# Sage layer behind the second layer's sums, and gathers issued half a round ahead of the maxima

## What is computed

```python
h = jnp.maximum(_layernorm(x), 0.0);  x = x + _L0_gnn_ref(h, adj, ...)   # GAT: 8 heads, then one output head
h = jnp.maximum(_layernorm(x), 0.0);  x = x + _L1_gnn_ref(h, adj, ...)   # GraphSAGE with the maximum over neighbours
h = jnp.maximum(_layernorm(x), 0.0);  x = x + _L2_gnn_ref(h, adj, ...)   # GAT, 4 heads
h = jnp.maximum(_layernorm(x), 0.0);  x = x + _L3_gnn_ref(h, adj, ...)   # mean over neighbours

# _L1_gnn_ref, the layer that the change is about
adj_ns = adj * (1.0 - eye)                       # no self loops
mx = where(adj_ns > 0, h[:, None], -1e30).max(axis=2)
neigh_agg = where(has_neigh, mx, h)              # a node without neighbours takes its own row
out = h @ W_self + b_self + neigh_agg @ W_neigh + b_neigh
out = relu(layernorm(out) * gamma + beta)
```

## Time and profile before

| | before |
|---|---|
| median of 3 runs | 9122.6 us (9110.27 to 9135.99) |
| the profiled execution, its own time | 9111.52 us |
| its span | 9109.8 us |
| busy PE, DVE, ACT, POOL | 5148.5, 5894.4, 4402.1, 5128.1 us |
| waits of PE's sage transposes for the maxima | 1096.9 us in 6 |
| POOL: gathers into G, into best | 1416 x 1061 ns, 1024 x 1068 ns |
| POOL: fetches of indices | 433 x 599 ns |

### The profile page before, as it was taken

The page is one execution under the profiler, slowest core; times in us unless marked ns, Lnnn a source line. Parts: engine busy times, 40 slices in busy tenths (PEclk is TensorE's granted clock), DMA queues, the critical chain, the costliest instruction groups (busy, mean ns, idle before and its releaser), DMA issues.

```text
span 9109.8 us, 178961 instructions
## 1 busy us (share of the span) xinstructions
PE 5148.5 (57%) x60584; PEld 4779.8 (52%) x60584; DVE 5894.4 (65%) x7002; ACT 4402.1 (48%) x3608; POOL 5128.1 (56%) x5234
## 2 busy tenths in 40 slices
PE   3673750365765668365865667556845667362026
PEld 3672750364755557363865567555745567361025
DVE  5874860386867788486867687687847688581024
ACT  5644730165635566165735566356715566160034
POOL 0004777377764677377764677276764677377630
PEclk9885875687877878687987888788877888686568
DMA  2114332234332533135322433234322433132210
GB/s 99 43 34 124 66 66 25 46 69 113 61 63 65 122 65 80 19 76 133 67 62 66 119 66 83 58 75 101 69 48 66 120 65 80 54 55 58 23 26 29
DMA packets 307180, 629.05 MB, mean 69 GB/s; under 512 B 113553, under 2 KB 165906, under 8 KB 270610
## 3 DMA queue, kind: packets, MB, share of 16 engines
q0 software_dynamic: 91936, 161.87, 16.9%
q1 hardware_dynamic: 212354, 456.38, 14.2%
q10 hardware_dynamic: 2160, 0.06, 0.0%
HBM read 506.89 MB, written 111.15 MB: 68 GB/s over the span
## 4 chain that ended last, share of the span: by engine, by line
POOL 20%; issue 16%; DVE 14%; PE 13%; DMA 8%; ACT 4%; POOLq 2%; DVEq 2%; ACTq 1%; SPq 0%
DMA G<-table,idx 6%; POOL G L552 6%; POOL best L552 5%; PE ps L1413 4%; POOL best L538 4%; PE ps L1386 3%; PE ps L1415 2%; POOL best L535 2%; DVE keys L1077 2%; POOL G L535 2%; ACT Pbuf L689 1%; PE ps L1438 1%; DVE key L1067 1%; POOL best L537 1%; ACT Hn L689 1%
## 5 line engine op out<-in xcount | busy, mean ns | idle before, releaser
L552 POOL DMA_INDIRECT G<-table,idx x1416 | 1502.7, 1061 | 508.5 <-issue 452.7
L1415 PE MATMUL ps<-Hn,AT 128*128 128x99 bf16 x12288 | 1774.5, 216 | 0.0
L1415 PE MATMUL ps<-X,AT 128*128 128x99 bf16 x12288 | 1735.0, 214 | 52.6 <-issue 52.6
L544 POOL DMA_DIRECT2D idx<-lists x433 | 259.3, 599 | 2445.9 <-issue 1964.9
L689 ACT ACTIVATE Hn<-Rb,q 128x2048 int8<-128x2048 f32 x768 | 1485.4, 1988 | 86.6 <-PE ps L1415 82.1
L689 ACT ACTIVATE Pbuf<-Rb,q 128x2048 int8<-128x2048 f32 x768 | 1487.8, 1987 | 18.2 <-PE ps L1415 15.6
L552 POOL DMA_INDIRECT best<-table,idx x1024 | 1093.7, 1068 | 319.4 <-issue 309.3
L1415 PEld LDWEIGHTS ps<-X,AT 128*128 128x128 fp8e4 x12288 | 1243.2, 101 | 57.6 <-issue 57.6
L1415 PEld LDWEIGHTS ps<-Hn,AT 128*128 128x128 fp8e4 x12288 | 1256.5, 102 | 0.0
L1413 PE MATMUL ps<-X,Hn 128*128 128x198 bf16 x6144 | 933.6, 268 | 567.6 <-DVE Hn L937 358.6
L1413 PE MATMUL ps<-Hn 128*128 128x198 bf16 x6144 | 960.3, 272 | 433.0 <-DVE Zs L957 236.0
(11 more groups left out here) (186 smaller groups left out, 11171.7 us busy)
## 6 DMA issues: line engine op xcount, KB each, us to landing
Rb<-in_adj SPq DMA_DIRECT2D x128, 1024.0 KB, 6.3
Rb<-rrows SPq DMA_DIRECT2D x104, 1024.0 KB, 6.3
bytes_A<-A SPq DMA_DIRECT2D x128, 256.0 KB
bytes_AT<-AT SPq DMA_DIRECT2D x128, 256.0 KB
AT<-bytes_AT SPq DMA_DIRECT2D x128, 256.0 KB, 3.6
AT<-bytes_A SPq DMA_DIRECT2D x128, 256.0 KB, 4.6
G<-table,idx POOLq DMA_INDIRECT x1416
h<-Hn SPq DMA_DIRECT2D x16, 1024.0 KB, 4.1
```

The source lines that it names most:

```text
L544: pool.dma_start(idx[:, slot, :], lists[bass.ds(r, 1)].rearrange("o p k -> (o p) k")).then_inc(idx_in[slot], 16)
L552: pool.indirect_dma_start(out=dst[:, k, :], out_offset=None, in_=table, in_offset=bass.IndirectOffsetOnAxis(ap=idx[:, slot, k:k + 1], axis ...
L1415: ins = pe.matmul(both[:, 0, 0:G], A8[:, jb, at], v[:, 0:G], start=False, stop=jb == T - 1, skip_group_check=True)
```

## The change

Two things change together.

In GpSimd's program `best` now takes the rows of every round, and `G`, half as wide, holds the maxima. Indices of a list are fetched in two transfers of four columns. A tile's rounds run by halves: wait for a half's four gathers (`landed`), fetch the same half's indices of the next list, take the half's maximum into `G` (the first half of a tile is a copy), then wait for those indices and issue the half's next four gathers (`ask`). The next list may be the next tile's first. The last tile of a graph runs its further rounds without this lead. The tree has two steps (2 and 1).

In `beside` the sage pairs come behind all 16 steps of the second layer's sums on PE (`sage`). On DVE the pairs' sums are handed to `finish`, which does one behind each of its operations from the third on; `statistics(1)` comes next, then the sage statistics as a loop, then `joined`. On ACT the exponential of `finish` stands behind the fourth of the eight sage copies, and `norm(1)` ahead of the sage norms. The three parts of the list stand behind steps 1, 2 and 3. The diff, cut to its core; the removed lines of `tile` are those printed above.

```diff
-        G = sb("G", [P, KEYS, F])
-        idx = sb("idx", [P, 2, KEYS], U32)
+        G = sb("G", [P, KEYS // 2, F])
+        idx = sb("idx", [P, KEYS], U32)
...
-            def fetch(r, slot):
+            def half(part):
+                return slice(part * (KEYS // 2), (part + 1) * (KEYS // 2))
+            def fetch(r, part):
                 plain(pool)
                 pool.wait_ge(list_in, r * 16 + 32)
-                pool.dma_start(idx[:, slot, :], lists[bass.ds(r, 1)].rearrange("o p k -> (o p) k")).then_inc(idx_in[slot], 16)
-            def rows_of(fetched, slot, dst):
+                pool.dma_start(idx[:, half(part)], lists[bass.ds(r, 1), :, half(part)].rearrange("o p k -> (o p) k")).then_inc(idx_in[part], 16)
+            def ask(r, part):
                 plain(pool)
-                pool.wait_ge(idx_in[slot], fetched * 16)
+                pool.wait_ge(idx_in[part], r * 16 + 16)
                 settle(pool)
-                for k in range(KEYS):
+                for k in range(part * (KEYS // 2), (part + 1) * (KEYS // 2)):
                     pool.indirect_dma_start(
-                        out=dst[:, k, :], out_offset=None, in_=table,
-                        in_offset=bass.IndirectOffsetOnAxis(ap=idx[:, slot, k:k + 1], axis=0)).then_inc(got[k], 16)
+                        out=best[:, k, :], out_offset=None, in_=table,
+                        in_offset=bass.IndirectOffsetOnAxis(ap=idx[:, k:k + 1], axis=0)).then_inc(got[part], 16)
+            def landed(r, part):
+                plain(pool)
+                pool.wait_ge(got[part], r * 64 + 64)
...
             def tile(b, t, last):
                 lo, hi = number(b, t), number(b, t + 1)
+                v = Chain(pool, merged, lo * MERGE, MERGE)
+                for part in range(2):
+                    landed(lo, part)
+                    if not last:
+                        settle(pool)
+                        fetch(lo + 1, part)
+                        plain(pool)
+                    if part == 0:
+                        settle(pool)
+                        v(pool.tensor_copy(G[:, :, :], best[:, half(0), :]))
+                    else:
+                        greater(v, G[:, :, :], best[:, half(1), :])
+                    if not last:
+                        ask(lo + 1, part)
+                settle(pool)
+                pool.sem_inc(merged, MERGE - v.n)
                 with pool.Fori(lo + 1, hi) as r:
+                    w = Chain(pool, merged, r * MERGE, MERGE)
                     if last:
+                        for part in range(2):
+                            fetch(r, part)
+                        for part in range(2):
+                            ask(r, part)
+                    for part in range(2):
+                        landed(r, part)
+                        if not last:
+                            settle(pool)
+                            fetch(r + 1, part)
+                            plain(pool)
+                        greater(w, G[:, :, :], best[:, half(part), :])
+                        if not last:
+                            ask(r + 1, part)
+                    w.end()
                     settle(pool)
                 v = Chain(pool, tree, (b * T + t) * TREE, TREE)
+                for width in (2, 1):
+                    greater(v, G[:, 0:width, :], G[:, width:2 * width, :])
                 settle(pool)
+                v(pool.tensor_copy(Agg[:, bass.ds(t, 1), :].rearrange("p o f -> p (o f)"), G[:, 0, :]))
                 v.end()
                 settle(pool)
...
-                fetch(number(b, 0), 0)
+                first = number(b, 0)
+                for part in range(2):
+                    fetch(first, part)
+                for part in range(2):
+                    ask(first, part)
                 with pool.Fori(0, T - 1) as t:
                     tile(b, t, False)
...
                 if b is not None:
                     prepare(LB, b)
                 if other is not None:
-                    sage_operands(other)
+                    sage_operands(other, range(T // 4))
+                if b is not None:
+                    elu_exp(LB, b, 0)
+                if other is not None:
+                    sage_operands(other, range(T // 4, T // 2))
+                if b is not None:
+                    norm(1, b, X, Hn, ACT.Relu)
+                if other is not None:
                     norm(4, other, Y, Y, ACT.Identity)
                     norm(2, other, X2, Hn2, ACT.Relu)
-                if b is not None:
-                    elu_exp(LB, b, 0)
-                    norm(1, b, X, Hn, ACT.Relu)
...
-            def finish(L, hn, lone):
+            def finish(L, hn, lone, between):
                 s, C = S[L], L.C
+                waiting = list(between)
+                def beside_it():
+                    if waiting:
+                        waiting.pop(0)()
...
                 v(dve.tensor_tensor(Z[:, full * w:], Z[:, full * w:], ps[:, full, 0:T * C - full * w], ALU.add))
+                beside_it()
                 v(dve.reciprocal(rden[:, :], zt[:, :, L.D]))
+                beside_it()
                 v(dve.tensor_tensor(o, o, rden[:, :].rearrange("p (t o) -> p t o", o=1).broadcast_to([P, T, L.D]), ALU.mult))
...
                 v(dve.tensor_tensor(X[:, :, :], X[:, :, :], Hn[:, :, :], ALU.add))
+                beside_it()
                 v.end()
+                while waiting:
+                    beside_it()
...
             def beside(b, other):
-                rest_of = []
-                between = [] if other is None or b is None else list(zip((0, 1, 2), list_tile(b, LIST_LB)))
-                if other is not None:
-                    for p in range(T // 2):
-                        between.append((p + 4, lambda p=p: sage_sums(other, p)))
-                        between.append((p + 5, lambda p=p: sage_statistics(other, p)))
-                    between.append((T // 2 + 4, lambda: rest_of.append(deviations(4, other))))
-                    between.append((T // 2 + 5, lambda: rest_of[0]()))
+                products = [] if other is None else [lambda p=p: sage_sums(other, p) for p in range(T // 2)]
                 if b is None:
-                    for at, work in sorted(between, key=lambda part: part[0]):
+                    for work in products:
                         work()
                 else:
                     prepare(LB, b)
-                    weigh(LB, 0, (b + 1) * 16, slice(0, 1), b, between)
+                    weigh(LB, 0, (b + 1) * 16, slice(0, 1), b,
+                          () if other is None else list(zip((1, 2, 3), list_tile(b, LIST_LB))))
+                    finish(LB, b, lone, products)
+                    statistics(1, b, X)
                 if other is not None:
+                    plain(dve)
+                    dve.wait_ge(M["sage"]["ev"], other * T + (T + 2))
+                    statistics(4, other, Y)
                     joined(other)
-                if b is not None:
-                    finish(LB, b, lone)
-                    statistics(1, b, X)
...
-            def sage_step(b, jb):
-                if jb == 1:
-                    sage_arrived(b)
-                if 2 <= jb < T // 2 + 2:
-                    sage_product(b, jb - 2)
-                if 1 <= jb < T // 2 + 1:
-                    sage_turned(b, jb - 1)
-            def sums(L, hn, other):
+            def sage(b):
+                sage_arrived(b)
+                for p in range(T // 2):
+                    sage_turned(b, p)
+                    sage_product(b, p)
+            def sums(L, hn):
...
                 if b is None:
-                    for jb in range(T // 2 + 2):
-                        sage_step(other, jb)
+                    sage(other)
                     return
                 prepare(LB, b, xc, None)
                 plain(pe)
                 pe.wait_ge(S[LB]["v"], (b + 1) * PREP_CHAIN)
-                sums(LB, b, other)
+                sums(LB, b)
+                if other is not None:
+                    plain(pe)
+                    pe.wait_ge(S[LB]["hsc"], b + 1)
+                    sage(other)
```

More of the change, by code:

```diff
@@ L190, in build @@
         bytes_AT = nc.dram_tensor("bytes_AT", [B * T, P, N], U8, kind="Internal").ap()
-        lists = nc.dram_tensor("lists", [ROUNDS + 2, P, KEYS], U32, kind="Internal").ap()
+        lists = nc.dram_tensor("lists", [ROUNDS + 4, P, KEYS], U32, kind="Internal").ap()
         h0 = nc.dram_tensor("h0", [P, T * F], F32, kind="Internal").ap()
@@ L248, in build @@
         idx_in = [sem("idx_in0"), sem("idx_in1")]
-        got = [sem(f"got{s}") for s in range(KEYS)]
+        got = [sem(f"got{s}") for s in range(2)]
         merged = sem("merged")
@@ L260, in build @@
         out_done = sem("out_done")
-        LN_CHAIN, LV_CHAIN, POOL_CHAIN, MERGE, TREE = 7, 12, 4, 6, 10
+        LN_CHAIN, LV_CHAIN, POOL_CHAIN, MERGE, TREE = 7, 12, 4, 6, 7
         PREP_CHAIN, EXPS, PAIRS = 9, 4, T // 2
@@ L587, in tile @@
```

(27 more changed lines are left out.)

10 lines of the change are left out of this document (removed).

## The result

The median is 9067.9 us against 9122.6: a ratio of 0.9935, 95% interval 0.991 to 0.9959. The change is faster by 0.65%, where 1.6% was forecast; the profiled execution spans 9061.2 us against the 8960 of the sum.

A forecast was written before the change was run, and what follows sets the result against it. No engine was near full; the longer of GpSimd's gather loop and the other engines' main loop bounds each turn. 1676 + 40, turns of 5983, then 53, 805 + 40 and 363 total 8960; forecast 8975 us, range 8850 to 9200.

The forecast's parts named there:

- first E: End of graph 0's gather on GpSimd, forecast at 1676 + 40 us.
- the turns: Six stretches from graph to graph, each as long as the longer of GpSimd's and the other engines' loop: together 5983 us.
- The two loops: GpSimd's gather plus idle time, beside the other engines' work until TensorE asks again; nearly equal, the longer bounds.
- the gathers' +40: GpSimd's gathers in each graph: 40 us longer, 15 to 70 with both bounds.
- the main loop's +10: Other engines' work per graph: 57 us more ahead of TensorE's asking, 47 less behind its start; grows by 10.
- Sage part, gather loop: From a gather's end to the next graph's first fetch: 53 us in place of 125, so 72 us less.
- Sage part, main loop: The 16 second-layer sums move ahead of TensorE's wait for the maxima: +57 us ahead of it, -47 behind.
- The gather part: GpSimd's tiles, all graphs: 368 us added, 300 of landing waits saved, 64 and 177 for later landings; sum 309.
- A quiet tile: GpSimd's tile of two rounds: 2.65 us longer, from gaps, one more fetch, the copy and entering the inner loop.
- The gather that keeps its length: Rival: GpSimd's gathers do not grow, the other engines' work mostly bounds; total 8790 us; chance 0.14.
- The fetch behind the gathers: Rival: index fetches land behind gathers and halves wait for them; 80 us a graph or more, 9239 and up; chance 0.24.
- slow in the sums: Rival: TensorE at 1.2 GHz in twelve second-layer sum steps, twice 3.57 us each; total 9124 us, no change; chance 0.10.

The follow-up runs named there:

- Sage part alone: Only the moved Sage work of the change, over the GpSimd program of the kernel before: 8893.4 us, ratio 0.9728.
- whole early lists: Changed kernel with two list buffers, a round's eight indices fetched in one transfer as soon as a buffer is free: 8854.4 us, ratio 0.969.
- early halves: Changed kernel with two list buffers and early fetches, each half's four indices in a transfer of their own: 8846.5 us, ratio 0.9676.
- GpSimd's part alone: Only the new GpSimd program of the change, with the Sage work left as in the kernel before: 9339.1 us, ratio 1.022.

## Why the forecast was too low by 93 us

The sum was short by 101 us of span: -14 at the first E (graph 0's gather grew by 27 us, not 40), +104 in the turns, +11 behind the last E. The two loops were the right picture, and the forecast of where TensorE would still wait came true: 39 and 36 us in the turns of 1019 and 1047, 4 and 0 in those of 961 and 971. What failed are two terms, the gathers' +40 and the main loop's +10.

The turns split like this. In the five that the gather loop ended, they are 72 us over the sum: 56 by their gathers, which grew by 47, 56, 63, 41 and 50 us where 40 stood, and 17 by the idle stretch, less 1 where the sum went by the main loop. The sixth, which the main loop ended, is 33 over. But the loops end so close together that each term alone would have moved the turns: with the forecast's main loops and the measured gather loops they sum to 6055, with its gather loops and the measured main loops to 6047, against 5983.

- **Sage part, gather loop: right to a few us.** 55 to 60 us from the later of the two loops' ends to the next fetch, against 53.
- **Sage part, main loop: mis-sized.** "The main loop grows by 10" nearly holds without GpSimd beside it (13). Beside it the loops are 981 to 1018 where 961 to 992 stood in the sum: on average 29 us more than before. TensorE asks 72 to 77 us after the first weighing, as forecast (73); the first sign of the third layer follows 108 to 112 us after the start, not 103; and the stretch from there to the next first weighing, which the sum took over unchanged, grew from 807 to 816 us on average (755 and 757 without GpSimd's work). The step of 3.57 us from graph 0, where GpSimd is idle, held beside GpSimd too: the last steps of the other graphs take 3.57 as well. The failure lies behind it: the sum treated VectorE's instructions as fixed while GpSimd's work beside them changed.
- **The gather part: right on average, wrong where it counts and in composition.** 43 us a graph against 40 over all eight, but 51 in the five that end turns, and 27, 27 and 33 in graphs 0, 4 and 7; why it is so uneven, no run shows. The forecast had some 120 us of added idle time and 189 of added busy time (106 of fetches, 83 of copies) over eight graphs. Measured: 12 us less idle time, 355 more busy time. The waits for landings went as it said, 390 us (its 300 are these less the gaps that stay); the waits for lists that came were 465, not 241; the other gaps shrank by some 90 where I let them grow by some 270. And no term held that the gathers take longer, which is 126 us, or the maxima, 40 with the copies above their forecast.
- **A quiet tile was right.** A quiet tile of two rounds, from its first fetch at 1566.96 to the next tile's at 1610.30, takes 43.3 us, the 41.3 of before (1384.89 to 1426.21) plus 2.0, against the 2.65 of the working; the gap between a maximum and the gathers behind it is 0.82:

```profile
1566.96 0.62 POOL L547 DMA_DIRECT2D idx<-lists  x1 [2.65 <-issue]
...
1577.26 1.26 POOL L538 TENSOR_TENSOR G<-G,best 128x512 f32<-128x512 f32 x1
1579.34 1.00 POOL L555 DMA_INDIRECT best<-table,idx  x1 [0.82 <-POOL G L538]
...
1610.30 0.62 POOL L547 DMA_DIRECT2D idx<-lists  x1 [2.65 <-issue]
```

- **The rivals.** The gather that keeps its length was priced at 8790; the nearest kernel, the Sage part alone, came to 8893. Of the 111 us between the two in span, 61 lie in its turns, 33 in the first and the last gather and 12 in the tail. The fetch behind the gathers is real, 36 us a graph, but below its 80. TensorE was not slow in the sums (3.57 us a step).
- **The tail** grew by 20 us, not 8. At the last graph's Sage step the granted clock stayed at the lower of its two levels: changed kernel (columns as in the earlier trace rows)

```profile
8686.00:8711.00 25.00, 18.61 (x77) 16.04 (x78) 2.54 (x6) 4.18 (x7) 0.07 (x1) 0.50 0.00 1
```

and the kernel with whole early lists, the same 25 us:

```profile
8481.00:8506.00 25.00, 14.52 (x96) 12.35 (x96) 4.64 (x13) 4.78 (x8) 0.27 (x1) 0.89 0.00 1
```

That kernel's tail is 365 us, as forecast (363), against 375. The kernel before, from which the 21.3 us of the Sage chain were read, had 0.84 in these 25 us. The other kernels with the Sage work behind the sums agree: tails of 375 and 371 us at 0.50 and 0.51 (Sage part alone, early halves), of 365 at 0.84 (without maxima). In the changed kernel and in the one with whole early lists TensorE was idle for over 420 us before; why the clock rose early in one and not in the other stays open.

What stays open too is why the rewrite adds 68 us to the main loop when its maxima are as many as before. VectorE is busy 6024 us with GpSimd's part alone and 5894 before, 6067 in the changed kernel and 5896 with the Sage part alone. The 128 new copies are not it: in the changed kernel the VectorE instructions that overlap most with them are only 15 us longer than without GpSimd. Those that overlap most with the subtractions and additions of 512 columns (lines 535 and 538) are 603 us longer, and 457 with the Sage part alone, though they are about as many (1104 and 1141). Which VectorE instruction a maximum falls beside differs between the programs, but no run settles that this is all of it.

## What to carry to other kernels

Where two loops of nearly the same length run side by side on engines that slow each other, price a change of one loop by what it does to the other loop's instructions too: here 377 of the 5997 us of six main loops go when GpSimd's maxima go. Price each turn by itself, since an average hides it: the gathers grew by 43 us on average, and by 51 where it counted. A lead in asking for data is worth only what the list of what to ask for allows: a small transfer issued right behind gathers landed 1.3 us later than one issued after a pause, so the half-round lead turned waits for rows into waits for lists, and two list buffers, not finer transfers, took them away. And before two halves of a change are shipped together, run each alone: here one was worth 2.7% and the other cost 2.2%.

## What the hardware showed that was not expected

- GpSimd's computing instructions lengthen VectorE's (a cast of 8 columns 172 to 443 ns on average, a mask of 512 columns 689 to 892); its gathers hardly do (187 and 689). The Trainium skill ("SBUF — State Buffer", SBUF: two separate sides) describes a port pair that VectorE's instructions with two inputs and GpSimd's instructions share as an exclusive lock, and the trace agrees in so far as the masks, with two inputs, shrink back when the maxima go. The cast, which has one input, grows more than the masks, 2.6 times; whether the other case of that section, a fast mode of VectorE, holds for it, no row here shows.
- The other way round, a gather's issue takes longer beside VectorE's long instructions. While the second layer's weighings run, in the changed kernel:

```profile
L555 POOL DMA_INDIRECT best<-table,idx x21 | 32.5, 1548 | 9.7 <-issue 4.9 <-POOL G L538 3.4 <-DMA idx<-lists 1.4
```

against 0.94 us in a quiet stretch. With the moved Sage work more gathers meet weighings: 74 lie mostly beside one (1.68 us on average, the others 1.10), 15 before (1.93 and 1.06). By these means that is 43 us against 13, an estimate, so it accounts for some 30 of the 126 us by which the gathers grew.
